# Two linear layers with gathered low-rank adapters: a first block on another queue, a finer warm-up, a last store in two halves

## What is computed

```python
# layer 0: adapter_mapping = itok_B_0_23; layer 1: adapter_ids = itok_B_6_15
x = x + x @ W.T + b + 2 * (x @ lora_As[i0]) @ lora_Bs[i0]
x = x + x @ base_weight.T + base_bias + (x @ lora_A_w[i1].T) @ lora_B_w[i1].T
```

## Time and profile before

| | |
|---|---|
| median of three runs | 284.68 us (284.08, 284.68, 284.77) |
| profiled execution, its own time | 284.42 us |
| its span, first to last instruction | 282.8 us |
| PE busy | 278.3 us (98%) |
| DVE, ACT, POOL busy | 215.2, 102.3, 19.3 us |
| PE idle before its first matmul | 1.7 us |
| last PE matmul starts | 279.70 us |

### The profile page before, as it was taken

The page is one execution under the profiler, slowest core; times in us unless marked ns, Lnnn a source line. Parts: engine busy times, 40 slices in busy tenths (PEclk is TensorE's granted clock), DMA queues, the critical chain, the costliest instruction groups (busy, mean ns, idle before and its releaser), DMA issues.

```text
span 282.8 us, 3853 instructions
## 1 busy us (share of the span) xinstructions
PE 278.3 (98%) x1319; PEld 224.5 (79%) x1319; DVE 215.2 (76%) x318; ACT 102.3 (36%) x141; POOL 19.3 (7%) x45
## 2 busy tenths in 40 slices
PE   7999999999999999999999999999999999999995
PEld 5888888888868887877888878888878888878885
DVE  5789999999899899967975873865873875865413
ACT  4565464262965574322331231141221131321100
POOL 3333200400000001000000100000000000000000
PEclk9999999999999999999999999999999999999999
DMA  6997000100365400451622802712701712212002
GB/s 217 391 409 309 31 1 2 57 19 0 129 230 211 139 14 19 158 185 76 206 74 76 261 37 75 236 46 80 249 37 74 239 43 93 75 39 86 25 37 111
DMA packets 13095, 33.92 MB, mean 120 GB/s; under 512 B 2149, under 2 KB 2405, under 8 KB 13078
## 3 DMA queue, kind: packets, MB, share of 16 engines
q1 hardware_dynamic: 11906, 31.60, 31.6%
q0 software_dynamic: 1024, 2.10, 2.3%
q10 hardware_dynamic: 148, 0.00, 0.0%
HBM read 22.09 MB, written 11.60 MB: 119 GB/s over the span
## 4 chain that ended last, share of the span: by engine, by line
PE 98%; DVE 0%; issue 0%
PE bank L1227 18%; PE bank L1228 18%; PE bank L1229 18%; PE bank L1065 9%; PE bank L1069 9%; PE bank L1070 9%; PE bank L1258 3%; PE bank L1234 3%; PE bank L1083 1%; PE bank L1105 1%; PE bank L1097 1%; PE bank L1099 1%; PE bank L1098 1%; PE bank L1085 1%; PE bank L1084 1%; PE bank L1167 1%
## 5 line engine op out<-in xcount | busy, mean ns | idle before, releaser
L1227 PE MATMUL bank<-ops,late 128*128 128x512 f32 x192 | 75.5, 393 | 0.0
L1228 PE MATMUL bank<-ops,late 128*128 128x512 f32 x192 | 74.9, 390 | 0.0
L1229 PE MATMUL bank<-ops,late 128*128 128x512 f32 x192 | 74.8, 389 | 0.0
L1069 PE MATMUL bank<-ops 128*128 128x512 f32 x112 | 43.8, 391 | 0.0
L1070 PE MATMUL bank<-ops 128*128 128x512 f32 x112 | 43.6, 390 | 0.0
L1227 PEld LDWEIGHTS bank<-ops,late 128*128 128x128 f32 x192 | 36.1, 188 | 9.5 <-issue 2.1
L1229 PEld LDWEIGHTS bank<-ops,late 128*128 128x128 f32 x192 | 36.1, 188 | 7.7
L1228 PEld LDWEIGHTS bank<-ops,late 128*128 128x128 f32 x192 | 36.1, 188 | 7.4
L1065 PE MATMUL bank<-ops 128*128 128x512 f32 x112 | 41.1, 401 | 0.0
L484 ACT CAST late<-rows 128x512 fp32r<-128x512 f32 x24 | 14.7, 622 | 52.3 <-DVE rows L762 26.0
L484 ACT CAST late<-raw_a 128x512 fp32r<-128x512 f32 x24 | 14.8, 624 | 30.6 <-PE bank L1234 21.1
(11 more groups left out here) (153 smaller groups left out, 379.4 us busy)
## 6 DMA issues: line engine op xcount, KB each, us to landing
raw_a<-xT SPq DMA_DIRECT2D x16, 512.0 KB, 4.8
out<-raw_a SPq DMA_DIRECT2D x27, 256.0 KB, 2.0
a<-rb_rows SPq DMA_DIRECT2D x8, 392.0 KB
raw_a<-W1T SPq DMA_DIRECT2D x2, 1024.0 KB, 12.6
raw_b<-W SPq DMA_DIRECT2D x2, 1024.0 KB, 16.3
rb_rows<-b_hl SPq DMA_DIRECT2D x3, 512.0 KB
rb_rows<-late SPq DMA_DIRECT2D x3, 512.0 KB
raw_a<-U SPq DMA_DIRECT2D x4, 256.0 KB, 4.4
```

What stands on the lines that cost most here:

```text
L1069: mm(bank[:, :], left(u, 0, k, m), op_k(v, 1, k), start=False, stop=False, skip_group_check=on_top)
L1227: mm(bank[:, :], hi, t_op(t, 0, k), start=(start and k == 0), stop=False, skip_group_check=not start)
L1228: mm(bank[:, :], hi, t_op(t, 1, k), start=False, stop=False, skip_group_check=not start)
L1229: last = mm(bank[:, :], lo, t_op(t, 0, k), start=False, stop=(k == KH - 1), skip_group_check=not start)
```

## The change

There are three parts. V11's block 0 is issued by ACT, as the first thing that ACT does, and no longer by SP as its second load. The warm-up's zeros are written on 256 columns, and 16 matmuls of 256 columns are made of them. The last store (the second half of 256 columns) is cut by rows: SP stores rows 0 to 63, ACT stores rows 64 to 127, each after the same wait.

```diff
-WARM = 8
+WARM = 16
...
+        def store_last(queue, n, part, done):
+            at = n * HALF // 2
+            queue.dma_start(out[(B - 1) * T + part.start:(B - 1) * T + part.stop, HALF + at:HALF + at + HALF // 2],
+                            c12[(B - 1) % 2][part, at:at + HALF // 2]).then_inc(last_stored[done], DMA)
...
             for k in range(KH):
                 for q, src in (("u11", U11), ("v11", V11)):
-                    sp.dma_start(raw_k(q, k), src[k, :, :]).then_inc(first_landed[q][k], DMA)
+
+                    if k or q == "u11":
+                        sp.dma_start(raw_k(q, k), src[k, :, :]).then_inc(first_landed[q][k], DMA)
...
-            for n in range(2):
-                at = n * HALF // 2
+            for n, part in ((0, slice(0, P)), (1, slice(0, P // 2))):
                 sp.wait_ge(made["c12"], B + n)
-                sp.dma_start(out[(B - 1) * T:(B - 1) * T + P, HALF + at:HALF + at + HALF // 2],
-                             c12[(B - 1) % 2][:, at:at + HALF // 2]).then_inc(last_stored[n], DMA)
+                store_last(sp, n, part, n)
...
-            for n in range(2):
+            for n in range(3):
                 sp.wait_ge(last_stored[n], DMA)
...
+            act.dma_start(raw_k("v11", 0), V11[0, :, :]).then_inc(first_landed["v11"][0], DMA)
             act.dma_start(idx[0:1, B:2 * B], idx1).then_inc(idx_landed, DMA)
...
+            act.wait_ge(made["c12"], B + 1)
+            store_last(act, 1, slice(P // 2, P), 2)
...
-            nc.vector.memset(c_rows[:, 0:HALF].bitcast(F32), 0.0).then_inc(warm_set, 1)
+            nc.vector.memset(c_rows[:, 0:2 * P].bitcast(F32), 0.0).then_inc(warm_set, 1)
...
-                mm(banks[7][:, :], c_rows[:, 0:P], c_rows[:, 0:HALF], start=True, stop=True)
+                mm(banks[7][:, 0:2 * P], c_rows[:, 0:P], c_rows[:, 0:2 * P], start=True, stop=True)
```

More of the change, by code:

```diff
@@ L191, in lora_pair @@
         stored = {q: sem(f"stored_{q}") for q in ("c11", "c12", "c21", "c22")}
-        last_stored = [sem(f"last_stored{n}") for n in range(2)]
+        last_stored = [sem(f"last_stored{n}") for n in range(3)]
         ident_made = sem("ident_made")
```

## The result

Over 16 runs the change has a median of 286.01 us (284.23 to 286.35), the kernel before, over 16 runs beside it, 284.31 us (283.73 to 284.94). The prediction was 284.6 us in a range of 283.7 to 285.4, with 0.07 on slower; it was wrong.

The account below looks back on a forecast made before the run. PE was taken to bound the kernel. U11's landing +0.16, warm-up 0 and last store -0.08 summed to +0.08 us, put on the four executions' mean of 284.49: 284.6 us, range 283.7 to 285.4.

Parts of the forecast that it names:

- The bound: Whole kernel: PE never runs dry, so only its useful start, its first matmuls' speed and the tail move the end.
- Part 1, U11's landing: Start: U11's block 0 lands 0.3 us later, bounds 0 and 0.62 by DVE's start; costs +0.16 us, at most +0.33.
- the second cast bound by the first one's end: Start, ACT: second cast starts where the first ends, so V11's landing has no more than some 0.03 us on the path.
- Part 1, POOL: Gathers: index rows land about 0.45 us later and POOL's eight gathers shift as much; slack 1.5 us, so no cost.
- Part 2, "I take 0": Warm-up: PE starting 0.21 us sooner is worth 0 through the clock; bounds nothing and a gain of 0.10 us.
- its rival: Warm-up to useful work: a 0.74 us gap makes PE start anew, the clock rising at 11.88; 286.5 us, chance 0.07.
- Half a microsecond more is little: Warm-up: the argument against the longer gap, 0.74 us where 0.2 did no harm, undoing the warm-up.
- Part 3: Last store: -0.08 us, most from a shorter issue with 64 rows; bounds -0.15 and +0.30.
- The bound of +0.30: Last store: ACT's store starts late, as its first issue took 0.30 us more than its second; 284.95 us, chance 0.11.
- The sum: Whole kernel: 0.16 + 0 - 0.08 = +0.08 us on the profiled execution's 284.42 us, giving 284.50.

Follow-up runs that it names:

- fill19: The whole change with 19 zero matmuls of 256 columns in place of 16; 284.60 us against 284.36 for the kernel before (ratio 0.9998).
- store_sp2: The kernel before with the last store as two halves of 64 rows, both issued by SP; run once, span ends 3.2 us after DVE's last add.
- gap6: The kernel before with 6 warm-up matmuls of 512 columns in place of 8, nothing else; 285.14 us against 284.41 (ratio 1.0013).
- after_c: The change as it is, timed again beside other kernels on one chip; 285.35 us against 284.48 for the kernel before (ratio 1.0028).
- warm_only: The kernel before with only the warm-up changed, to 16 matmuls of 256 columns; 284.37 us against 284.36 (ratio 0.999).
- change17: The whole change with 17 zero matmuls in place of 16; 284.42 us against 284.48 for the kernel before (ratio 1.0011).

## Why the prediction was wrong

- **The bound, right.** PE is the path, and start, clock and tail are all that moved.
- **Part 1, U11's landing, right in kind.** I took 0.3 us, half of the way to an even split; DVE's identity came 0.46 us later (4.27 against 3.81), which was inside the bounds. The blocks of two queues share the engines nearly evenly: landings of 3.3 and 3.4 us from the same issue time. The Trainium skill, "DMA: Bandwidth & Descriptors", section "Issuing engines are not separate DMA queues", has them interleave on the same engines; these landings agree. Useful work moved by 0.38 only, since the two casts now start 0.52 us apart (4.60 and 5.12) and not 0.61. This shows a misread: I had called the second cast bound by the first one's end. Casts can overlap by 0.1 us, and before it was V11 that held the second back.
- **Part 1, POOL, wrong and harmless.** The gathers came 1.3 us later, not 0.45 (last issue 17.54 against 16.23), and POOL's first read of an index came at 5.2 where it was 3.8; that the index rows queued behind V11's bytes is my guess. ACT read them at 23.55, and no wait of it appears.
- **Part 2, "I take 0", the step that failed.** Its sum treated the rise as fixed at 7.78 or moving with PE's start. I did see the gap and priced its rival at 286.5 with a chance of 0.07; it came out at 286.1 in 60% of the runs. That the price was so near is partly luck: it had the rise at 11.88 and a loss of 1.78 us for it, where the profiled execution has 9.43 and 0.61 (0.79 with the later start counted as the prediction did), and it took the store for a gain. The forecast rested on one execution per kernel, in which the rise happened to be at 7.78: nothing showed how far it moves from run to run. The traces now have it from before 5.4 up to 10.5. The spread of the four times shown was no measure of that. "Half a microsecond more is little" was an opinion with no row behind it.
- **Part 3, wrong in sign.** I took -0.08, mostly from a shorter issue; it was +0.41. I had drawn a line from one row (0.22) to 128 rows (0.40) and read 64 rows off it; they cost more than 128. The bound of +0.30 came from another cause, ACT's first use, and was still too small. The Trainium skill (the same page, section "Rules for kernel authors") advises against two transfers to disjoint halves; where it speaks of nothing gained, the runs show a loss.
- **The sum.** +0.16 + 0 - 0.08 for the profiled execution should have read +0.38 + 0.61 + 0.41. The 0.38 counts in full here because I now count the slow matmuls apart; on the prediction's scale, where the rise stays, it would have been 0.20.

## What to carry to other kernels

Let the warm-up last until the first useful matmul can start; when an edit moves that start, the warm-up's length moves with it. Three zero matmuls more cost nothing here that shows (useful work at 5.87 in fill19, 5.88 in the change), and a gap of 0.9 us or more made about half of the executions late. Where the clock's rise is inside the measured time, one trace shows one draw: compare the distribution of a dozen runs, by span as well as by time, and count slow matmuls. A load that gates the first work should not share the engines with its neighbour, and a small store is not made faster by halving its rows.

## What I had not expected of the hardware

- An issue of 64 rows of 1 KB takes 0.54 and 0.59 us on SP in store_sp2, and 0.56 on ACT in the change; of 128 such rows it takes 0.33 on SP. Why stays open.
- The time outside the span has two levels, 1.5 to 1.8 and 2.2 to 2.8 us. The upper one came in 66 of 183 runs of the kernels with 7 or 8 zero matmuls of 512 columns, and in none of 146 runs of the others, gap6 with 6 of them included. Why stays open.
- The rise of TensorE's clock differs by some 5 us and more between executions of nearly the same program, while the granted clock reads 1.00 in each: while its zeros ran in after_c, before 5.4 us in warm_only, 7.78 before, 9.43 in the change, 10.46 in change17. What decides it within a kernel was not found. That a gap in PE's work makes the late rises common is shown by the counts; that the gap is what undid the earlier work in any one trace is inferred.
- Two ACT casts of 128x512 can start 0.52 us apart though each record lasts 0.62.
